# Cross-attention in a decoder layer: every second copy of the value sums out of PSUM goes to VectorE

## What is computed

```python
def _L0_xattn_ref(q, k, v, start_pos, mask):
    xq = q.reshape(b, s, 8, 4, 16)              # b = 8, s = 128
    xk, xv = k.reshape(b, t, 8, 16), v.reshape(b, t, 8, 16)
    scores = jnp.einsum('bsgrd,btgd->bgrst', xq, xk) / math.sqrt(16)
    probs = jax.nn.softmax(scores + mask, axis=-1)
    out = jnp.einsum('bgrst,btgd->bsgrd', probs, xv)
    return out.reshape(b, s, 512)
x = _layernorm(x + _L0_xattn_ref(x, ctx_1024, ctx_1024, 0, mask_SxS2_ff0), axis=-1)
```

## Time and profile before

| what | us |
|---|---|
| median of three runs | 1655.9 |
| the profiled execution, whole | 1657.49 |
| its span (first to last instruction) | 1655.7 |
| attention stage, first scores to first feed-forward matmul | 1387.55 to 1498.92 |
| one batch (four steps) in the middle of it | 13.94 |
| TensorE busy in the span | 1620.0 |
| VectorE busy in the span | 1194.6 |
| ScalarE busy in the span | 950.9 |

### The profile page before, as it was taken

The page is one execution under the profiler, slowest core; times in us unless marked ns, Lnnn a source line. Parts: engine busy times, 40 slices in busy tenths (PEclk is TensorE's granted clock), DMA queues, the critical chain, the costliest instruction groups (busy, mean ns, idle before and its releaser), DMA issues.

```text
span 1655.7 us, 25594 instructions
## 1 busy us (share of the span) xinstructions
PE 1620.0 (98%) x9120; PEld 1273.1 (77%) x9120; DVE 1194.6 (72%) x2366; ACT 950.9 (57%) x1584; POOL 963.0 (58%) x727
## 2 busy tenths in 40 slices
PE   9999999999999999999999999999999998889998
PEld 7788888888888888888888888888888885444646
DVE  7767687767876786768686868586858679996433
ACT  6765376546744583558364837383738365995231
POOL 2977487657856694659474948494938563331000
PEclk9999999999999999999999999999999999999999
DMA  5432133213422241224131423141314172000000
GB/s 195 150 102 86 49 112 125 77 58 102 134 65 70 89 134 58 89 87 132 51 102 59 134 75 103 48 143 58 123 45 134 57 106 107 1 20 20 13 14 26
DMA packets 76547, 138.85 MB, mean 84 GB/s; under 512 B 6786, under 2 KB 13954, under 8 KB 76164
## 3 DMA queue, kind: packets, MB, share of 16 engines
q1 hardware_dynamic: 76420, 137.21, 26.2%
HBM read 134.55 MB, written 2.63 MB: 83 GB/s over the span
## 4 chain that ended last, share of the span: by engine, by line
PE 87%; DVE 9%; issue 1%; ACT 1%; DMA 1%; POOL 0%; SPq 0%; DVEq 0%; ACTq 0%; POOLq 0%
PE ps_hs L248 7%; PE ps_hs L250 7%; PE ps_hs L249 7%; PE ps_y L1197 7%; PE ps_gate L249 7%; PE ps_gate L248 7%; PE ps_gate L250 7%; PE ps_hs L1205 7%; PE ps_hs L1207 6%; PE ps_hs L1206 6%; PE ps_gate L1183 4%; PE ps_y L1483 3%; PE ps_hs L1445 3%; PE ps_dec L1445 3%; DVE conv L765 2%; DVE pr L1030 2%
## 5 line engine op out<-in xcount | busy, mean ns | idle before, releaser
L765 DVE SCALAR_TENSOR_TENSOR conv<-ps_hs,cw,conv 128x508 f32<-128x508 f32 (+2 forms) x432 | 320.3, 742 | 31.4 <-ACT conv L530 20.2
L394 POOL TENSOR_TENSOR cum_bc<-cum_bc,neg_cum 128x1024 f32<-128x1024 f32 x128 | 247.5, 1934 | 10.8 <-DMA cum_bc<-cum_scratch 0.2
L248 PE MATMUL ps_hs<-x_hi,w_hi 128*128 128x512 f32 x576 | 231.6, 402 | 0.0
L250 PE MATMUL ps_hs<-x_hi,w_lo 128*128 128x512 f32 x576 | 225.3, 391 | 0.0
L249 PE MATMUL ps_hs<-x_lo,w_hi 128*128 128x512 f32 x576 | 224.5, 390 | 0.0
L248 PE MATMUL ps_gate<-x_hi,w_hi 128*128 128x512 f32 x576 | 224.5, 390 | 0.0
L249 PE MATMUL ps_gate<-x_lo,w_hi 128*128 128x512 f32 x576 | 224.4, 390 | 0.0
L250 PE MATMUL ps_gate<-x_hi,w_lo 128*128 128x512 f32 x576 | 224.4, 390 | 0.0
L1205 PE MATMUL ps_hs<-wo_hi,g_hi 128*128 128x512 f32 x488 | 192.6, 395 | 1.9 <-DVE g_acc L877 1.1
L1206 PE MATMUL ps_hs<-wo_lo,g_hi 128*128 128x512 f32 x488 | 190.7, 391 | 0.0
L1207 PE MATMUL ps_hs<-wo_hi,g_lo 128*128 128x512 f32 x488 | 190.6, 391 | 0.0
(11 more groups left out here) (172 smaller groups left out, 3330.8 us busy)
## 6 DMA issues: line engine op xcount, KB each, us to landing
cum_bc<-cum_scratch SPq DMA_DIRECT2D x128, 512.0 KB, 4.1
w_raw<-w_in SPq DMA_DIRECT2D x145, 256.0 KB, 4.6
wo_raw<-w_out SPq DMA_DIRECT2D x64, 256.0 KB, 4.9
g_acc<-x_t SPq DMA_DIRECT2D x4, 512.0 KB, 5.6
acc<-x_nat SPq DMA_DIRECT2D x1, 2048.0 KB, 10.0
k_rep<-ctx_t SPq DMA_DIRECT2D x8, 256.0 KB, 12.6
out<-y_out SPq DMA_DIRECT2D x8, 256.0 KB, 2.0
wg_sb<-w_gate SPq DMA_DIRECT2D x1, 1792.0 KB, 16.9
```

What stands on the lines that cost most here:

```text
L248: eng.matmul(ps, whi, xhi, start=(k == 0), stop=False)
L250: return eng.matmul(ps, wlo, xhi, start=False, stop=(k == n - 1))
L394: gp.tensor_tensor(part, part, start.broadcast_to([P, 2, HB, SEQ]), ALU.add).then_inc(S["bc_ok"], 1)
L765: v.scalar_tensor_tensor(out=dst, in0=src, scalar=cw[:, at, TAPS - 1 - n:TAPS - n], in1=dst, op0=ALU.mult, op1=ALU.add).then_inc(S["tap"], 1)
```

## The change

`keep_values(n)` for odd n from 1 to 13 leaves ScalarE and becomes a VectorE instruction. ScalarE keeps n = 0, 2, ..., 14 and, in the feed-forward part (L735), n = 15. Seven of sixteen copies move. On VectorE the copy stands in steps 8, 12, ..., 32, behind the eight masks of the step and ahead of `attended`. Waits, buffers and the semaphore counts are the same.

```diff
-                if i % 2 == 0 and i >= 6:
+                if i % KD == 2 and i >= 6:
                     keep_values((i - 6) // 2)
...
+            def keep_values(n):
+
+                dve.wait_ge(S["pv_ps"], 4 * n + 4)
+                need(dve, S["back_ps"], n - 1)
+                v.tensor_copy(pvs[n % 2][:, :], PV_PS[:, :]).then_inc(S["pvs_ok"], 1)
+
             def attended(b, o):
...
                 if i == 1:
                     inverses(1, 1, others)
+                if i % KD == 0 and i >= 8:
+                    keep_values((i - 6) // 2)
                 if i % 2 == 0 and i >= 8:
                     n = (i - 8) // 2
```

## The result

Six runs of the changed kernel gave a median of 1663.97 us (1661.21 to 1666.35), six of the kernel before beside them 1656.03 us (1655.17 to 1657.99). The ratio is 1.004, 95% interval 1.003 to 1.005: 7.9 us slower, where 2.9 us were forecast. The profiled execution took 1663.7 us with a span of 1661.9.

The account below looks back on a forecast made before the run. The prediction took a TensorE-VectorE ring of waits, 13.94 us a batch, as the bound. Its terms, 3.0 - 0.65 + 0.60 + 0 = 2.95 us, on 1655.9 gave 1658.8 us (+0.18%), range 1655.3 to 1661.5.

Parts of the forecast that it names:

- The ring: Attention stage, steps 8 to about 23: TensorE and VectorE wait in turn, 13.94 us a batch; five copies add 3.0 us.
- The price of the copy: Each moved PSUM copy on VectorE: about 684 ns long, 0.60 us to the next start, against 0.48 on ScalarE.
- Nothing back from ScalarE in the ring: Up to step 23, ScalarE's lost copy work only makes it wait longer for `keep_queries`: worth nothing.
- 0.65 us back at step 27, 0.60 paid at step 28: VectorE's 0.65 us wait for copy L699 before `x2_low` vanishes; step 28's moved copy adds 0.60 us.
- Nothing at step 32: Last moved copy: taken as 0, bounds 0 and 0.6 us, since TensorE still has eight transposes to do.
- The sum, 2.95 us: Whole attention stage: 3.0 - 0.65 + 0.60 + 0 us longer, bounds 1.0 and 4.8 us.
- the clock falls more often: Rival: TensorE's idle before `turn_queries` grows to about 1.8 us and lowers its clock; 1660.5 to 1667.3 us, chance 0.11.
- The rival's price, 1.7 us a fall: TensorE at the low clock for about 3.4 us, half the work lost: 1.7 us for each fall.
- The range: Whole kernel: 1655.3 to 1661.5 us, covering no change, the forecast with its bounds, and one clock fall with some spread.
- VectorE has room: Rival: VectorE's 1.35 us of idle a batch hides the copy; 1655.9 us within 0.8, chance 0.15.
- ScalarE is the pace: Rival: ScalarE bounds the stage, so seven copies fewer bring 3.4 us; 1652.5 us, chance 0.05.
- the second rival: The prediction's closing name for the rival of clock falls, to be shown by new falls between 1400 and 1490 us; chance 0.11.

Follow-up runs that it names:

- relief: The kernel before with six of the seven moved copies left out altogether, VectorE unchanged; 1655.0 us against 1656.2 beside it, ratio 0.9993.
- filler: The changed kernel with four more identity transposes on TensorE in each of five waits for `attended`; 1658.19 us, ratio 1.0009 to the kernel before.
- after_warm: The changed kernel with four identity transposes before `attended` in five steps, plus 36 and 12 in two long idles; 1657.65 us, ratio 1.0008 to the kernel before.
- early: The kernel before with `attended` of steps 8, 12 to 32 ahead of its step's eight masks, copies still on ScalarE; 1658.56 us, ratio 1.0013.

## Why the prediction was wrong, point by point

- *The ring* (`attended`, `turn_queries`, scores, value sums, `turn_probs`, three steps of VectorE): right. 0.60 us a batch, no cover by VectorE's idle (1.15 us before L1039 in step 17, as before), waits of TensorE 8.5 us in total; batch 14.54 us.
- *The price of the copy*: right. 687 ns, 0.60 to the next start.
- *Nothing back from ScalarE in the ring*: right, by relief.
- *0.65 us back at step 27, 0.60 paid at step 28*: the sum of the two, -0.05, was -0.21 in the piece from step 24 to 28, by filler and after_warm against the runs without falls; a little more came back than I took.
- *Nothing at step 32*: too low. The piece from 28 to 32 was longer by 0.46 us in after_warm and 0.73 in the changed kernel, against 0 taken and 0.6 as its upper bound; the changed kernel has 0.60 less behind it, so that 0.13 is left there, and 0.45 in after_warm.
- *The sum, 2.95 us*: near what was found without falls, 2.8 us by the pieces of the changed kernel and 2.97 with the clock held full, of which 0.6 is taken and not measured. That the second agrees so closely is luck: against the terms of the forecast the ring gave 0.27 less there (0.53 a batch), steps 24 to 28 0.16 less, and step 32 0.45 more. The terms that stand in it are not what failed.
- *The step that failed*: the sum took TensorE's work behind the longer idle at full clock, so new falls stood in it at nothing, and were left to the rival "the clock falls more often" with a chance of 0.11, on the ground that one idle of 1.83 us in the trace had not cost the clock. One such case says that it can pass, not that it does. The runs showed three falls of 1.64 us each, 4.9 of the 7.7 us in the stage: of eight idles of 1.81 and 1.82 us in two profiles of the changed kernel, six were followed by a fall. The same trace also had the row that spoke for it, 2.11 us with a fall, and the change made four idles of 1.81 us in a ring that had had none above 1.22. The rival's price, 1.7 us a fall, was right (1.64); three falls at it make 2.9 + 5.1 = 8.0 us, against 7.7 in the stage and 7.9 and 5.4 by the medians of the two comparisons. The range ended at one fall and a spread, 1661.5, and left out two and more.
- The rule of the Trainium skill beside that rival (TensorE: Matmul & The Clock Gate, section A second HAM failure mode) is that short frequent idles between groups of matmuls let the clock swing. The changed kernel's trace agrees, with three falls and recoveries within 55 us; early's, with four idles of 1.78 us and no fall, does not.
- "VectorE has room" and "ScalarE is the pace" are both out, the one by the batch of 14.54 us, the other by relief.
- Two slips: the earlier trace rows has the clock during the idle of 1.83 us, which ends at 1478.20, and not behind it (there it is full too, 1.00 from 1478 to 1482); and "the second rival", at the end of the prediction, is the first of its list.

## What to carry to other kernels

When an edit lengthens one wait of TensorE, the longer idle has a second price beside its own length, the clock for the work behind it, and in a ring of waits that work is on the path. If the trace has idles about as long as the new one will be, some with a fall behind them and some without, take a fall as about even (here 9 of 23), and multiply by the number of idles.

An engine's idle time hides added work only if the work stands behind the instruction that others wait for: here the same copy, three instructions further back, cost nothing that the runs could tell. And the cheapest test for the clock is a few matmuls with no reader in the idle. Four in each of five idles gave 5.8 us back to the changed kernel, and 48 in two long idles 1.9 us to the kernel before.

## What the runs showed of the hardware that I had not expected

In early the add of L1053, 0.42 us in the ring of the kernel before, took 0.97 us in four batches, always where a GpSimd instruction had just started:

```profile
1436.84 1.04 POOL L478 TENSOR_TENSOR k_bd<-k_rep,kbd_mask 128x512 f32<-128x512 f32 x1 [3.27 <-PE ps_dec L1364]
...
1437.20 0.97 DVE L1053 TENSOR_TENSOR acc<-acc,att 128x256 f32<-128x256 f32 x1
```

GpSimd's multiply ran until 1437.88; the add, issued at 1437.20, ended at 1438.17, 0.29 us later. 0.55 us of a VectorE instruction with two operands in SBUF is waiting. By the Trainium skill (SBUF — State Buffer, section Who interferes with whom) such an instruction needs the port that it shares with GpSimd, and whichever of the two comes second waits until the first is through; the rows agree. In the kernel before the two did not meet in the ring; they did once behind it, where the add at 1481.00 took 0.88 us. In early the meeting stands in steps 12, 16, 20 and 24 and not in step 8. The batch from step 8 took 13.84 us, those from 12 and 16 14.38, so by these rows, as an estimate, it accounts for the 0.54 us between them, and for 0.55 of the 1.78 us for which TensorE stood there.
